# More groups of probability transposes made by two row tiles of TensorE, in an attention and feed-forward kernel

## What is computed

```python
x = x + xattn0(layernorm(x), ctx)      # 16 heads of 64
x = x + ffn0(layernorm(x))             # 8-bit activations, ternary weights, depthwise conv
x = x + xattn1(layernorm(x), ctx)      # 16 heads of 16, RMS norm and rotary embedding on q and k
x = x + ffn1(layernorm(x))
# in each xattn, per head:
attn = softmax(q @ k.T * scale)        # 112 x 375
out  = attn @ v
```

## Time and profile before

| | |
|---|---|
| median of 3 runs | 2393.19 us (2389.81 to 2396.25) |
| the profiled execution | 2391.42 us |
| its span from first to last instruction | 2389.5 us |
| PE busy | 2311.8 us, 97% |
| DVE, ACT, POOL busy | 68%, 63%, 68% |
| full turns (L424) | 322 groups, 1932 transposes |
| row turns (L414) | 190 groups, 2280 transposes and 190 tiny products |
| chain that ended last | PE 93% |

### The profile page before, as it was taken

One profiled execution on the slowest core, in us unless ns is written; L12 is line 12 of the kernel. 1 busy time (PEld: TensorE's weight loads), 2 busy tenths in 40 slices (PEclk: granted clock), 3 DMA queues, 4 the chain that ended last, 5 costly groups with the idle time before them and its releaser, 6 DMA issues.

```text
span 2389.5 us, 60414 instructions
## 1 busy us (share of the span) xinstructions
PE 2311.8 (97%) x20064; PEld 1771.2 (74%) x20064; DVE 1627.5 (68%) x3996; ACT 1511.1 (63%) x4305; POOL 1628.5 (68%) x1830
## 2 busy tenths in 40 slices
PE   6999999999999999999999999999999999999578
PEld 5777777777777777777777777777777777777336
DVE  6666666776666667666666776666667666666785
ACT  4666666666666666666666666666666666666356
POOL 3776776676767767666776666777767676776507
PEclk9999999999999999999999999999999999999689
DMA  4100000000000000000000000000000000000202
GB/s 155 35 11 10 10 8 10 2 10 10 10 10 8 10 2 10 10 10 10 10 8 7 5 10 10 10 10 8 10 2 10 10 10 10 9 3 2 55 10 63
DMA packets 31197, 37.04 MB, mean 16 GB/s; under 512 B 3284, under 2 KB 29636, under 8 KB 31172
## 3 DMA queue, kind: packets, MB, share of 16 engines
q1 hardware_dynamic: 31172, 36.71, 5.3%
HBM read 29.36 MB, written 7.34 MB: 15 GB/s over the span
## 4 chain that ended last, share of the span: by engine, by line
PE 93%; DVE 3%; issue 2%; POOL 2%; ACT 1%; DMA 0%; POOLq 0%; SPq 0%; ACTq 0%; DVEq 0%
PE ps L339 25%; PE ps L400 17%; PE pt L424 11%; PE pa L436 7%; PE pt L414 5%; PE ps L383 5%; PE pa L471 5%; PE pa L451 4%; PE pa L339 2%; PE pt L339 2%; PE pa L566 1%; PE pa L606 1%; PE pt L591 1%; PE ps L464 1%; DVE th L1378 1%
## 5 line engine op out<-in xcount | busy, mean ns | idle before, releaser
L1027 DVE TENSOR_REDUCE nmx<-ps 112x2 f32<-112x750 f32 x512 | 480.4, 938 | 198.2 <-PE ps L400 192.6
L1474 POOL TENSOR_TENSOR prob<-prob,rinv 112x375 f32<-112x375 f32 x512 | 405.5, 813 | 195.3 <-DVE rinv L1035 195.2
L1474 POOL TENSOR_TENSOR f1w_room<-f1w_room,rinv 112x375 f32<-112x375 f32 x512 | 404.8, 817 | 65.8 <-DVE rinv L1035 65.8
L750 ACT ACTIVATE room<-ps 128x375 f32<-128x375 f32 (+2 forms) x480 | 228.1, 489 | 307.1 <-PE ps L339 307.1
L750 ACT ACTIVATE probT<-pt 125x336 f32<-125x336 f32 (+1 forms) x512 | 243.0, 475 | 195.9 <-PE pt L414 141.7
L790 ACT ACTIVATE prob<-ps,nmx 112x375 f32<-112x375 f32 x512 | 290.4, 581 | 64.6 <-DVE nmx L1027 64.6
L790 ACT ACTIVATE f1w_room<-ps,nmx 112x375 f32<-112x375 f32 x512 | 291.7, 588 | 2.3 <-DVE nmx L1027 2.3
L1499 POOL TENSOR_TENSOR krs<-krs,nhalf 125x48 f32<-125x48 f32 x32 | 257.1, 8033 | 0.0
L400 PE MATMUL ps<-kT,q 64*112 64x375 f32 x1024 | 235.0, 518 | 1.0 <-ACT prob L790 1.0
L400 PE MATMUL ps<-room,q 64*112 64x375 f32 x1024 | 232.7, 519 | 2.6 <-ACT prob L790 1.9
L1018 DVE COPY probT<-pt 125x336 f32<-125x336 f32 x322 | 162.8, 506 | 96.6 <-PE pt L424 96.6
(11 more groups left out here) (263 smaller groups left out, 5270.5 us busy)
## 6 DMA issues: line engine op xcount, KB each, us to landing
craw<-in_ctx SPq DMA_DIRECT2D x32, 375.0 KB, 3.1
xin<-in_x SPq DMA_DIRECT2D x32, 112.0 KB, 2.0
x_rows<-x SPq DMA_DIRECT2D x32, 112.0 KB, 1.9
out<-probT SPq DMA_DIRECT2D x16, 224.0 KB, 2.4
room<-x_rows SPq DMA_DIRECT2D x1, 2576.0 KB, 12.4
stage<-in_f1w SPq DMA_DIRECT2D x2, 1024.0 KB, 5.2
stage<-in_wk SPq DMA_DIRECT2D x1, 1024.0 KB, 6.3
stage<-in_wv SPq DMA_DIRECT2D x1, 1024.0 KB, 8.9
```

What stands on the lines that cost most here:

```text
L750: return act.activation(dst, src, ACT.Copy)
L1027: top = dve.tensor_reduce(nmx[:, g:g + 2], ps[0:T, 2 * (i % 2):2 * (i % 2) + 2, 0:S], AX_X, ALU.max, negate=True)
L1474: pool.tensor_tensor(prob(i, n), prob(i, n), rinv[:, g:g + 1].to_broadcast([T, S]), ALU.mult).then_inc(s["normed"], 1)
```

## The change

`by_rows` loses its condition that i is odd. All groups are turned by rows but the last two of a part: groups 0 to 12 of MIDDLE instead of 1, 3, ..., 11, and groups 0 to 4 of OPENING and CLOSING instead of 1 and 3. The same function decides for the copies of ACT and DVE, so they follow. The very first turn of OPENING has no earlier copies to wait for, so its wait is left out.

```diff
         def by_rows(i, part):
 
-            return i % 2 == 1 and i + 1 + AHEAD < (G if part == MIDDLE else PAIRS)
+            return i + 1 + AHEAD < (G if part == MIDDLE else PAIRS)
 
@@
             def turn(i, part, b):
 
                 if by_rows(i, part):
-                    pe.wait_ge(s["pT_even"], at(i, part, b))
-                    pe.wait_ge(s["pT_odd"], at(i, part, b))
+                    if part != OPENING or i >= 1:
+                        pe.wait_ge(s["pT_even"], at(i, part, b))
+                        pe.wait_ge(s["pT_odd"], at(i, part, b))
                     pe.wait_ge(s["normed"], 2 * at(i, part, b) + 2)
                     pe.matmul(pt[:, 0, 511:512], identb[0:64, :], identb[0:64, 0:1], start=True, stop=True)
```

## The result

| | before | changed |
|---|---|---|
| median | 2394.72 us (2389.81 to 2396.68, 4 runs) | 2450.30 us (2446.28 to 2454.00, 4 runs) |
| profiled execution | 2391.42 us | 2454.0 us |
| span | 2389.5 us | 2452.2 us |

The ratio is 1.0239, with a 95% interval from 1.0227 to 1.0251: the kernel is 2.4% slower, 55.6 us by the medians. The forecast was 2434 us with a range from 2408 to 2450. Direction and mechanism hold; the loss is 15 us larger than forecast and the median stands 0.3 us outside the range.

The account below looks back on a forecast made before the run. PE, busy 97%, bounded the kernel; after the change the loop PE, row maxima, copy, PE would be longest. 2391.42 us profiled plus 40.9 us from 31 MIDDLE parts gave 2432.3, against the runs 2434 us, range 2408 to 2450.

Parts of the forecast that it names:

- What bounds it before: Full turn of even groups in a pair: waits 0.10 us for ACT's copy; DVE's later copy costs nothing.
- The transposes save nothing: Transposes of a changed turn: values follow 0.80 us after its start against 0.81, saving 0.01 us.
- The start of the even group's turn: Even group's row turn starts 0.23 us after DVE's copy ends, 0.24 us later than now; pair +0.23 us.
- Scores to copy end stay 2.30 us: In a pair, scores' start to end of DVE's copy, behind the row maxima: 2.30 us, unchanged.
- Group 0 gains nothing: First turn of MIDDLE: helps at first, but group 1's turn waits for DVE's copy; gain nothing, bound 0.34 us.
- Group 2: Turn of group 2 in MIDDLE: +0.08 us at its start, +0.09 us with the query transpose, +0.17 us in all.
- MIDDLE in all: Each MIDDLE part 1.32 us longer: five pairs at 0.23 us plus 0.17 us; 31 parts, 40.9 us.
- OPENING and CLOSING at nothing: Changed turns in OPENING and CLOSING: effect set at nothing, with 1 us to either side.
- Rival A: Wait for DVE's copy doesn't bind, one mode change less per pair: 45 us gained, 2348 us; chance 0.09.
- Rival B: Release costs 0.14 us, values follow after 0.70 us: +0.04 us a pair, 9 us, 2402 us; chance 0.08.
- Rival C: Weight loads behind late release not overlapped, values at 0.92 us: +0.35 us a pair, 63 us, 2456 us; chance 0.09.

Follow-up runs that it names:

- MIDDLE alone: Kernel before with the change in MIDDLE only, OPENING and CLOSING keeping row turns for odd groups only: 2442.46 us, ratio 1.0207; repeated, 2441.00 us, 1.0206.

## Why the prediction was right, and where it fell short

- **What bounds it before.** Right. Before, a full turn waits for ACT's copy (a shorter copy gains, halved maxima don't); DVE's copy is free there.
- **The transposes save nothing.** Right: the values follow 0.81 us after a row turn's start against 0.81 for a full turn; the forecast took 0.80.
- **The start of the even group's turn.** The mechanism is as forecast, with DVE's copy as releaser, and three edits bear it out: shorter maxima, a longer copy, more work on PE ahead of the turn. From copy end to start are 0.24 us, where 0.23 were taken. The pair grows by 0.24 to 0.25 us instead of 0.23 (4.06 to 4.07 against 3.82; in layer 0, 1103.08 to 1107.73, 4.65 against 4.41). In five pairs of 31 parts this is 2 to 3 us.
- **Scores to copy end stay 2.30 us.** Right: 1109.26 to 1111.56.
- **Group 0 gains nothing.** Right within 0.05 us, though the releaser behind it may be POOL and not DVE. **Group 2**: forecast +0.17; from the first scores of a part to its first values 5.25 us against 5.08 (1071.41 less 1066.33 before): +0.17. That is the sum of both groups: from the turn of group 1 to the values it is +0.22 (2.71 against 2.49), less the 0.05 of group 0. That the two together hit the number is in part luck.
- **Left out: what follows group 12.** Behind its values stands the full turn of group 13 with no scores between. It starts 0.14 us behind ACT's copy, which now comes later: 0.78 instead of 0.71 us behind the values. The next values come 3.72 instead of 3.61 us behind the last ones, 3 us in all. I had looked only at the row turns that follow.
- **MIDDLE in all.** 1.5 us a part instead of 1.32 (five pairs at 0.24 to 0.25, 0.17, 0.11): 46.4 us in the profile instead of 40.9. This term was undersized by an eighth.
- **OPENING and CLOSING at nothing.** This is the step that failed: "I set both at nothing, with 1 us to either side". In the medians the two ends took 5 to 8 us, all of it time at 1.2 GHz as far as the executions show. In the profiles OPENING took 4.8 us more from its first scores on, each time; CLOSING took 9.5, 1.5 and -0.3 us. Six more turns by rows cost nothing at the same clock; the length of the low-clock stretches was the term that was missing. The runs of before alone, 6.4 us apart, could have told that something varies by more than 1 us. Without this excess the changed kernel would stand at 2441.0 to 2442.5 us, as MIDDLE alone does, inside the range. What makes the stretches longer stays open.
- **Rival A.** Priced at 45 us of gain if DVE's copy ended 0.44 us sooner, at 1082.80. No run gave that, and none could: the copy would have to start at 1082.36, and the row turn that it copies ends at 1082.53. With the maxima halved it came 0.17 us sooner and the pair to 3.89, not 3.6. I had priced the removal of one wait without asking which is next. **Rival B** (a release of 0.14 us, values after 0.70 us) didn't happen: 0.24 and 0.81 were measured. **Rival C** (values at 0.92 us) didn't happen either.

## What to carry to other kernels

Where PE is busy 97% and every other engine under 70%, look at when single buffers come free before trusting that a new wait is covered: a turn that needs both banks at once is released by the later of two copies, and that one stood behind 0.94 us of other work. Two forms of the same step can cost PE the same and still differ in what they wait for; alternating them may be worth more than using the "better" one throughout. When a buffer hand-over is on the path, give its shorter part to the engine that is waited for, and try it: the gain was 0.5% for exchanging two banks. And a reordering that frees the copy must be priced by everything that stood ahead of it.

## What the runs showed of the hardware that was not expected

- From the end of DVE's copy to the tiny product of a row turn are 0.23 to 0.24 us: 0.24 in the changed kernel and with the exchanged banks, 0.23 with row turns for even groups. From the end of ACT's copy to a full turn are 0.14 us (1083.09 to 1083.23 before, 1121.37 to 1121.51 in the changed kernel).
- ACT's copy out of PSUM of 125 partitions takes 0.49 us for 384 elements a partition and 0.41 for 288; DVE's takes 0.54 and 0.44.
- After the same wait of PE in OPENING, the granted clock didn't fall in one profile (1.00), returned to 2.4 GHz within 4 to 7 us in others (0.97, 0.94) and after about 20 us in all three of the changed kernel (0.83), in nearly the same program. PE was busy for all of the 10 us from 50 to 60 us in these three, at a granted clock of 0.50. The cause stays open.
